# Two batches of chunks for the second normalisation of each local layer, with row statistics column-tiled on TensorE and sent through DRAM to all partitions

## Chip, cores, metric

One core of a Trainium2 chip. The metric is the time of one execution on the device, in microseconds (us). The kernel is a program written out by hand: each engine has its own list of instructions, and semaphores connect the lists.

## What is computed

The input x is (4, 1024, 128), so 4096 tokens of 128 channels. A feed-forward block of two local layers, a global attention block, and the same feed-forward block again:

```python
x = x + 0.5 * ffn(layernorm(x))        # two local layers
x = x + attn(layernorm(x))             # causal attention and a memory term
x = x + 0.5 * ffn(layernorm(x))        # the same two local layers
```

One local layer, of which there are four in one execution:

```python
h = shift_token(x)                     # upper 64 channels come from the token before
q, k, v = split(h @ wqkv); q, k = l2norm, scales, rotary_xpos
x = x + local_attention(q, k, v) @ wo  # windows of 64 tokens
h = shift_token(x)
h = (h - h.mean(-1)) / sqrt(h.var(-1) + 1e-5) * lg + lb
a, g = split(h @ w1 + b1)              # 341 hidden channels each
x = x + (a * gelu(g)) @ w2 + b2
```

The change is about the third line from the end of the second part: the mean and variance over the 128 channels of each token, between attention and the hidden layer ("the second normalisation").

## The kernel before

Activations lie channels-first, [128 channels, tokens], in `z_a` (`z_in`, the layer's input) and `z_b` (`z_out`, the sum after attention). Tokens are cut into 32 tiles of 128 (`TILE`, numbered 0 to 31 in a layer) and 8 chunks of 512 (`CHUNK`, numbered 0 to 7), so chunk m is tiles 4m to 4m+3.

`local_attention_pass` runs both layers of one feed-forward block. For tiles 0 to 27 a function `body(i, k)` on each engine interleaves stages of five different tiles: keys, queries and values of tiles ahead (L197 to L208), the softmax maxima on VectorE (L403), the exponentials on ScalarE (L330, eight a tile, called slots 0 to 7), the normalisation of the probabilities on GpSimd (L298), their transposes on TensorE (L249) with copies to SBUF (`probsT`, L351 on ScalarE and L416 on VectorE), the products with the values (L265), the head copy (L356), the output projection (L276), and the residual (L421, semaphore `z_done`). GpSimd also sums and scales the rotary parts (L285, L291), after which TensorE turns queries and keys of the tile (L219, semaphores `q_turned`, `k_turned`).

Tiles 28 to 31 are written out in `attention_end(layer)`, and there the second normalisation of all eight chunks is woven in by hand. This stretch is called the tail below. For each chunk:

- SyncE copies the shifted chunk from `z_out` to `ln_h` with two DMAs (`sp_ln_chunk`, L532 and L533); for chunk 7 VectorE and GpSimd copy the halves instead (`dve_ln_high` L519, `gp_ln_low` L525).
- TensorE multiplies by `K["centre"]`, identity minus 1/128, into a PSUM bank (L475, a full 128x512 f32 product: `pe_centre`).
- ScalarE squares that (L497), TensorE multiplies the squares by `K["mean"]`, all 1/128 (L490, `pe_var`), which gives the variance on all 128 partitions at once; ScalarE takes the logarithm (L503) and exp(-0.5 log) (L508); VectorE multiplies the centred bank by it into `z_in` (L512, `dve_ln_scale`).

After the tail come the eight chunks of the hidden layer: gate and value products (L592, L597), the rest of the hidden channels (L603, and L610 as two products on 64 columns each), Gelu on ScalarE (L630), `dve_hide` (L640), the down product (L621) and the sum on VectorE (L646). The first Gelu needs another table of activations, loaded by L979 behind the last exponential of the normalisation. Hidden-layer products wait for PSUM banks that Gelu and `dve_hide` release (`pe_await_bank`).

Each f32 product is two records (and two weight loads) in the profile. Engines take their lists in order: an instruction whose semaphore isn't there holds up all behind it on its engine.

Of the kernel before, what the change touches and what calls it, by code (L numbers as in the profile page):

```python
# [14 lines left out]
P = 128  # L15
# [83 lines left out]
LN_MOVES = ("ln_low", "ln_high")  # L99
MLP_SEMS = ("mlp_gate", "mlp_value", "mlp_gelu", "mlp_hidden", "mlp_down", "mlp_out")  # L100


LN_PAIRS = ((0, 1), (1, 0), (0, 1), (3, 4), (1, 0), (4, 3), (0, 1), (2, 7))
LN_BEHIND = {1: 0, 2: 1, 4: 2, 5: 3, 6: 4}
# [29 lines left out]
WOVEN = TILES - 4  # L134

# [4 lines left out]
def local_attention_pass(nc, C, K, W, probs, probsT, z_in, z_out, x, first):  # L140


    C.open(("pass_set", "ln_in0", "ln_in1", "ln_in2", "ln_in3", "hs_in0", "hs_in1", "hs_in2", "hs_in3", "v_in0", "v_in1", "v_in2", "v_in3"))
    with ExitStack() as ctx:
# [27 lines left out]
        ln_h, squares, rstd = ln[:, 0:4, :], ln[:, 4:6, :], ln[:, 6:8, :]  # L172
# [32 lines left out]
        def pe_project_values(pe, wait, i, k):  # L205
            wait("v_ready", i, k, 1)
            wait("z_done", i, k, 4)
            nc.tensor.matmul(ps[:, VB, :], hs[:, k % 4, :], W["wqkv"][:, i // B, 2 * INNER:3 * INNER], start=True, stop=True  # L208
                             ).then_inc(C["v_done"], 1)
# [242 lines left out]
        def ln_wait(eng, name, layer, m):  # L452
            eng.wait_ge(C[name], C.after(name, CHUNKS * (layer + 1) + m + 1))

        def ln_banks(layer, m):
            return FIRST_PAIRS[m % 3] if layer < 0 else LN_PAIRS[m]


        def pe_centre(pe, wait, layer, m):
# [4 lines left out]
            elif m == CHUNKS - 1:  # L464
                pe.wait_ge(C["ln_low"], C.after("ln_low", layer + 1))
                pe.wait_ge(C["ln_high"], C.after("ln_high", layer + 1))
            else:
                pe.wait_ge(C[f"ln_in{m % 4}"], C.after(f"ln_in{m % 4}", (32 if m % 4 == 3 else 64) * layer + 32 * (m // 4 + 1)))
                if m == 0:
                    wait("q_rotated", *t(layer, LAST))  # L470
                elif m == 3:
                    wait("max_done", *t(layer, LAST), 0, HEADS)
                else:
                    ln_wait(pe, "ln_log", layer, LN_BEHIND[m])
            nc.tensor.matmul(ps[:, centred, :], K["centre"][:, :], x[:, columns(m)] if layer < 0 else ln_h[:, m % 4, :],  # L475
                             start=True, stop=True).then_inc(C["ln_centred"], 1)

        def pe_var(pe, wait, layer, m):
# [5 lines left out]
            elif m == CHUNKS - 1:  # L484
                wait("heads_ready", *t(layer, LAST))
            elif m == 0:
                wait("k_squared", *t(layer, LAST))
            elif m != 3:
                ln_wait(pe, "ln_out", layer, LN_BEHIND[m])
# [3 lines left out]
        def act_ln_square(act, layer, m):  # L493
            ln_wait(act, "ln_centred", layer, m)
            if m >= 2:
                ln_wait(act, "ln_var", layer, m - 2)
            nc.scalar.activation(squares[:, m % 2, :], ps[:, ln_banks(layer, m)[0], :], ACT.Square).then_inc(C["ln_squared"], 1)  # L497

        def act_ln_log(act, layer, m):
            ln_wait(act, "ln_var", layer, m)  # L500
            if m >= 2:
# [13 lines left out]
        def dve_ln_high(dve, wait, layer):  # L515
            m = CHUNKS - 1
            wait("z_done", *t(layer, LAST))
            ln_wait(dve, "ln_centred", layer, m - 4)
            nc.vector.tensor_copy(ln_h[64:128, m % 4, :], z_out[64:128, columns(m, 1)]).then_inc(C["ln_high"], 1)  # L519

        def gp_ln_low(gp, wait, layer):
            m = CHUNKS - 1
            wait("z_done", *t(layer, LAST))
            ln_wait(gp, "ln_centred", layer, m - 4)
            nc.gpsimd.tensor_copy(ln_h[0:64, m % 4, :], z_out[0:64, columns(m)]).then_inc(C["ln_low"], 1)  # L525

        def sp_ln_chunk(sp, wait, layer, m):

            wait("z_done", *t(layer, 4 * m + 3))
            if m >= 4:  # L530
                ln_wait(sp, "ln_centred", layer, m - 4)
            sp.dma_start(ln_h[0:64, m % 4, :], z_out[0:64, columns(m)]).then_inc(C[f"ln_in{m % 4}"], 16)  # L532
            sp.dma_start(ln_h[64:128, m % 4, :], z_out[64:128, columns(m, 1)]).then_inc(C[f"ln_in{m % 4}"], 16)  # L533
# [55 lines left out]

        def pe_gate(pe, layer, c, j):  # L590
# [2197 lines left out]
```

## Time and profile before

| | us |
|---|---|
| three runs: median (lowest, highest) | 1970.66 (1968.64, 1971.12) |
| the profiled execution, its own time | 1968.74 |
| span of the profile | 1966.7 |
| busy: TensorE, VectorE, ScalarE, GpSimd | 1898.6, 1648.5, 1504.3, 915.3 |
| granted TensorE clock, mean | 0.986 |

The span runs from the first to the last instruction in the profile. 1968.74 is the time of that one execution; the difference of 2.0 us lies around the span. A busy TensorE isn't necessarily at its peak, as ends of products are modelled; where starts are compared, the distance between starts is the price of an instruction.

The four tails begin (first product of the normalisation) at 268.45, 589.43, about 1539 and 1860.08 us. The words "first tail" mean the one of 268.45.

### The profile page before, as it was taken

The numbers are of one execution on the slowest core, as the hardware profiler recorded it, in microseconds if no ns is written. First come the engines' busy times: TensorE is split into PE (matmuls) and PEld (weight loads), VectorE is DVE, ScalarE is ACT, GpSimd is POOL, SyncE is SP. The second block draws the span as 40 slices with busy tenths as digits, with TensorE's granted clock in tenths as the row PEclk, the third lists the DMA queues.
The fourth block names the chain that finished last, engine by engine and source line by source line (L and its number), as shares of the span: only waits on it lengthen the run. The fifth ranks groups of instructions, "written<-read, shape, count | busy, mean of one in ns | idle before, by whom it ended". The sixth has DMA issues, their size and how long they took to land. (4 is left out here: it accounts for less than half of the span.)

```text
span 1966.7 us, 53041 instructions
## 1 busy us (share of the span) xinstructions
PE 1898.6 (97%) x18494; PEld 1125.7 (57%) x18494; DVE 1648.5 (84%) x5474; ACT 1504.3 (76%) x4121; POOL 915.3 (47%) x548
## 2 busy tenths in 40 slices
PE   7999999999999989999999998899999999999998
PEld 3777763577775343434434367437777635777753
DVE  5999975899995679999999769779999659999955
ACT  5999994799997353777777754469999848999963
POOL 2788860588882040000000046337888406888800
PEclk9999999999999997999999999999999999999999
DMA  6222220112120040111111000002212201121201
GB/s 185 46 45 46 46 65 6 34 43 49 43 66 23 6 155 26 42 42 41 43 41 42 20 5 2 2 19 49 48 43 47 55 6 41 43 48 43 67 15 43
DMA packets 76107, 85.11 MB, mean 43 GB/s; under 512 B 17136, under 2 KB 50500, under 8 KB 75716
## 3 DMA queue, kind: packets, MB, share of 16 engines
q1 hardware_dynamic: 75647, 81.70, 16.6%
q8 instruction: 150, 2.46, 0.5%
q14 instruction: 114, 0.93, 0.2%
q10 hardware_dynamic: 196, 0.02, 0.0%
HBM read 21.16 MB, written 8.39 MB: 15 GB/s over the span
## 5 line engine op out<-in xcount | busy, mean ns | idle before, releaser
L330 ACT ACTIVATE probs<-probs,negmax 128x128 f32<-128x128 f32 x1024 | 399.9, 396 | 23.6 <-DVE negmax L403 22.5
L2165 ACT ACTIVATE gprobs<-ps_global 128x1024 f32<-128x1024 f32 (+3 forms) x384 | 291.4, 811 | 125.1 <-PE ps_global L1630 102.4
L285 POOL TENSOR_TENSOR rot<-rot 128x1024 f32<-128x1024 f32 x128 | 302.1, 2360 | 144.0 <-DVE rot L373 144.0
L291 POOL TENSOR_TENSOR qk<-rot,cnorm 128x1024 f32<-128x1024 f32 x128 | 243.7, 1904 | 120.2 <-POOL rot L285 92.3
L298 POOL TENSOR_TENSOR probs<-probs,iden 128x1024 f32<-128x1024 f32 x128 | 242.8, 1897 | 120.1 <-DVE iden L411 120.1
L1860 DVE TENSOR_REDUCE maxes<-ps_global 128x1 f32<-128x512 f32 (+2 forms) x384 | 222.1, 639 | 10.7 <-PE ps_global L1593 6.5
L403 DVE CUSTOM_DVE_ANT_0 probs<-ps_attn,masks 128x128 f32<-128x128 f32 x1024 | 226.0, 285 | 0.4 <-issue 0.3
L1588 PE MATMUL ps_global<-kq 48*128 48x512 bf16 (+3 forms) x768 | 196.7, 345 | 7.5 <-DVE maxes L1860 1.8
L330 ACT ACTIVATION_READ_ACCUMULATOR probs<-probs,negmax 128x1 f32 x1024 | 197.1, 192 | 0.0
L371 DVE TENSOR_TENSOR rot<-ps_attn,rotary 128x512 f32<-128x512 f32 x256 | 175.1, 684 | 2.1 <-PE ps_attn L197 1.5
L265 PEld LDWEIGHTS ps_attn<-probsT,v_first 128*64 128x64 f32 x2048 | 118.1, 136 | 98.1 <-ACT probsT L351 95.1
L2095 POOL CAST m_parts<-m_turn 32x128 bf16<-32x128 f32 x16 | 4.5, 280 | 363.6 <-DVE m_turn L1874 363.6
L1645 PE MATMUL ps_global<-gprobs,v_all 128*9 128x512 f32 (+3 forms) x1536 | 160.7, 490 | 1.7 <-ACT gprobs L2165 1.7
L249 PEld LDWEIGHTS ps_attn<-ident,probs 128*128 128x128 f32 x1024 | 117.7, 140 | 69.2 <-POOL probs L298 61.4
L630 ACT ACTIVATE ln<-ps_attn,vecs_sb 128x512 f32<-128x512 f32 (+2 forms) x96 | 65.6, 683 | 116.8 <-PE ps_attn L592 72.7
L379 DVE TENSOR_REDUCE ssq<-sq 128x16 f32<-128x1024 f32 x128 | 154.7, 1209 | 0.1
L1856 DVE CUSTOM_DVE_ANT_0 ps_global<-ps_global,later 128x384 f32<-128x384 f32 (+1 forms) x256 | 152.2, 653 | 2.7 <-PE ps_global L1588 1.7
L1588 PEld LDWEIGHTS ps_global<-kq 48*128 48x128 bf16 x768 | 58.8, 94 | 160.3 <-DVE maxes L1860 86.4
L1621 PE MATMUL ps_global<-kq 51*128 51x512 bf16 (+3 forms) x768 | 145.6, 329 | 2.3 <-ACT gprobs L2165 1.9
L219 PE MATMUL ps_attn<-ident,qk 128*128 128x128 f32 x1024 | 139.8, 279 | 5.9 <-POOL qk L291 3.9
L236 PE MATMUL ps_attn<-kT,qT 64*64 64x128 f32 x4096 | 141.3, 275 | 0.0
L265 PE MATMUL ps_attn<-probsT,v_first 128*64 128x64 f32 x2048 | 138.5, 230 | 0.7 <-ACT probsT L351 0.7
(220 smaller groups left out, 4599.4 us busy)
## 6 DMA issues: line engine op xcount, KB each, us to landing
v_first<-v_second SPq DMA_DIRECT2D x256, 128.0 KB, 2.3
hs<-z_a SPq DMA_DIRECT2D x256, 32.0 KB, 1.9
ln<-z_b SPq DMA_DIRECT2D x56, 128.0 KB, 2.4
kq<-split_scratch SPq DMA_DIRECT2D x64, 96.0 KB
kq<-split_scratch SPq DMA_DIRECT2D x64, 64.0 KB
split_scratch<-parts SPq DMA_DIRECT2D x8, 384.0 KB, 4.1
split_scratch<-gprobs SPq DMA_DIRECT2D x6, 384.0 KB, 4.1
x_tok<-in_x_dram SPq DMA_DIRECT2D x4, 512.0 KB, 6.5
```

Of the source, the lines that this page charges most:

```text
L265: last = nc.tensor.matmul(out[:, queries], v[:, k % 4, cols], probsT[:, 4 * e + pair, queries], start=True, stop=True, skip_group_check=True)
L285: nc.gpsimd.tensor_tensor(a, a, b, ALU.add).then_inc(C["rot_sum"], 1)
L291: nc.gpsimd.tensor_tensor(qk[:, k % 2, :].rearrange("p (h d) -> p h d", d=DH), rot_a[:, k % 2, :, :], cnorm[:, k % 2, :].unsqueeze(2).to_b ...
L298: nc.gpsimd.tensor_tensor(pr, pr, iden[:, k % 2, :].unsqueeze(2).to_broadcast([P, HEADS, SPAN]), ALU.mult).then_inc(C["probs_ready"], 1)
L330: last = nc.scalar.activation(probs[:, k % 2, slot, :], probs[:, k % 2, slot, :], ACT.Exp, scale=-1.0, bias=negmax[:, k % 2, slot:slot + 1 ...
L371: nc.vector.tensor_tensor(rot_a[:, k % 2, h0:h0 + HEADS, :], x, cos, ALU.mult)
L379: nc.vector.reduce_sum(ssq[:, k % 2, :], sq[:, :].rearrange("p (h d) -> p h d", d=DH), AX_X).then_inc(C["ssq_done"], 1)
L403: nc.vector.tensor_tensor_reduce(probs[:, k % 2, slot, :], ps[:, SB0 + slot // 4, (slot % 4) * SPAN:(slot % 4 + 1) * SPAN], K["masks"][:, ...
L1588: mm = nc.tensor.matmul(out, qs[buf][rows, p, tile_cols(t)], ks[buf][rows, p, CHUNK * c:CHUNK * c + w], start=True, stop=not masked_here, ...
L1645: mm = nc.tensor.matmul(ps[32 * h:32 * h + AD + 1, O0, t0 - CHUNK * c:CHUNK], v_all[:, S_TILES * (n // GROUPS) + s, GROUP * (n % GROUPS) + ...
L1860: nc.vector.reduce_max(maxes[:, n % 2, r, p0:p1, t, c], ps[:, bank_of(use), 0:len(both) * w].rearrange("q (p s) -> q p s", s=w), AX_X).the ...
L2165: nc.scalar.activation(probs[:, step % RING, 2 * p:2 * p + 2, 0:w], ps[:, S0 + 2 * p:S0 + 2 * p + 2, 0:w], ACT.Exp).then_inc(C["p2_exp"], 1)
```

## The change

Chunks 0 to 3 form batch 0, chunks 4 to 6 form batch 1 (`LN_BATCHES`). Chunk 7 keeps the old way (its source is now `last_h`). A batch goes so, b being its number:

1. Inputs. SyncE copies the shifted chunks to `inputs[m]`, for batch 0 while tiles 20 to 23 run, for batch 1 after tile 30's values, and there behind `k_turned` of tile 31, as the chunks lie in the buffer `qk`.
2. `pe_mean`: for each chunk a product with 32 columns of `K["mean"]`, each in its own quarter of the array's columns, all into one PSUM bank. Batch 0 in `body` of tile 26, batch 1 in the tail, between the transposed probabilities and the value products of tile 29.
3. `act_mean` copies the bank to SBUF; for batch 1 it stands ahead of slots 4 to 7 of tile 30's exponentials.
4. `sp_spread(…, 0)`: SyncE writes one row a chunk to DRAM, waits for it, and reads it back to all 128 partitions.
5. `centre_batch`: input minus mean, on VectorE for batch 0 (ahead of `dve_inv` of tile 29), on GpSimd for batch 1 (ahead of `gp_ln_low`).
6. `act_batch_square`, `pe_batch_var` (column-tiled again), `act_batch_log`, `act_batch_inverse`, once a batch.
7. `sp_spread(…, 1)` sends the inverse deviations the same way, and `dve_batch_scale` multiplies. Chunks 0 and 1 are scaled ahead of the residual of tile 31, chunks 4 to 6 inside the hidden layer, behind the first `dve_out`.

`first.gpsimd`, scaling of weights in the first pass alone, moves from the end of GpSimd's tail to behind tile 28's part of it. The core of the diff:

```diff
+LN_BATCHES = ((0, 1, 2, 3), (4, 5, 6))
+EARLY_MEAN = WOVEN - 2
+        def pe_mean(pe, wait, layer, b):
+            if b == 0:
+                bank = VB
+                wait("z_done", *t(layer, EARLY_MEAN - 1))
+            else:
+                bank = KB
+                wait("k_squared", *t(layer, LAST))
+            step_wait(pe, "lb_in", layer, b, moves_in(b), moves_in(b))
+            for n, m in enumerate(LN_BATCHES[b]):
+                last = nc.tensor.matmul(ps[32 * n:32 * n + 32, bank, :], K["mean"][:, 0:32], inputs[m], start=True, stop=True,
+                                        skip_group_check=True, tile_position=(0, 32 * n))
+            last.then_inc(C["lb_mean"], 1)
...
+        def centre_batch(eng, engine, layer, b):
+            step_wait(eng, "lb_spread", layer, b, spread_moves(b), 2 * spread_moves(b))
+            for m in LN_BATCHES[b]:
+                engine.tensor_tensor(inputs[m], inputs[m], spread[m], ALU.subtract).then_inc(C[f"lb_centred{b}"], 1)
...
+        def sp_spread(sp, wait, layer, b, what):
+            batch_wait(sp, ("lb_copied", "lb_rstd")[what], layer, b)
+            n = len(LN_BATCHES[b])
+            out = ln_rows[layer, b, what, 0:n, :]
+            sp.dma_start(out, rows_of[b][0:32 * n - 31:32, :]).then_inc(C[f"lb_rows{b}"], 16)
+            step_wait(sp, "lb_rows", layer, b, 16 * (what + 1), 32)
+            if b == 0:
+                sp.dma_start(ln[:, 4:8, :], out.partition_broadcast(P)).then_inc(C["lb_spread0"], 16)
+                return
+            if what == 0:
+                wait("ssq_done", *t(layer, LAST))
+            sp.dma_start(qk_flat[:, 3, :], out[0, :].partition_broadcast(P)).then_inc(C["lb_spread1"], 16)
+            sp.dma_start(sq_flat[:, :, :], out[1:3, :].partition_broadcast(P)).then_inc(C["lb_spread1"], 16)
...
 # TensorE, attention_end
                 pe_transpose_probs(pe, wait, *t(layer, 29), True)
-                pe_var(pe, wait, layer, 1)
+                pe_mean(pe, wait, layer, 1)
                 pe_values(pe, wait, *t(layer, 29), True)
...
-                pe_centre(pe, wait, layer, 7)
-                ln_wait(pe, "ln_out", layer, 6)
+                wait("max_done", *t(layer, LAST), 0, HEADS)
                 pe_gate(pe, layer, 0, 0)
-                pe_var(pe, wait, layer, 7)
                 pe_gate(pe, layer, 0, 1)
+                pe_batch_var(pe, wait, layer, 1)
                 wait("p5_read", *t(layer, LAST))
                 pe_value(pe, layer, 0, 0)
+                pe_centre(pe, wait, layer, LAST_CHUNK)
                 wait("p6_read", *t(layer, LAST))
                 pe_value(pe, layer, 0, 1)
+                batch_wait(pe, "lb_log", layer, 0)
                 pe_wide(pe, layer, 0)
+                pe_var(pe, wait, layer, LAST_CHUNK)
...
 # VectorE, attention_end
                 dve_clip_norm(dve, wait, *t(layer, 31))
+                centre_batch(dve, nc.vector, layer, 0)
                 dve_inv(dve, wait, *t(layer, 29))
...
                 dve_probsT(dve, wait, *t(layer, 31))
-                dve_ln_scale(dve, layer, 3)
-                dve_ln_scale(dve, layer, 4)
+                dve_batch_scale(dve, layer, 0)
+                dve_batch_scale(dve, layer, 1)
                 dve_residual(dve, wait, *t(layer, 31))
```

What this does to the order of instructions, in the first tail. TensorE from the output projection of tile 28 on (L276 before, L295 now), before:

```order
L276 MATMUL ps_attn<-oT,wo_sb 128x128 x4
L475 MATMUL ps_attn<-ln,centre 128x512
L249 MATMUL ps_attn<-ident,probs 128x128 x8
L490 MATMUL ps_attn<-ln,mean 128x512
L265 MATMUL ps_attn<-probsT,v_first 64x64
```

and now (L268 is what L249 was, L284 what L265 was):

```order
L295 MATMUL ps_attn<-oT,wo_sb 128x128 x4
L268 MATMUL ps_attn<-ident,probs 128x128 x8
L504 MATMUL ps_attn<-qk,mean 32x512 x3
L284 MATMUL ps_attn<-probsT,v_first 64x64
```

One chunk's centring and variance gave way to the three means of batch 1, on whose inputs the value products of tile 29 now wait.

TensorE at the start of the hidden layer, before (L592, L597, L603 are gate, value and the wide rest):

```order
L276 MATMUL ps_attn<-oT,wo_sb 128x128 x4
L490 MATMUL ps_attn<-ln,mean 128x512
L475 MATMUL ps_attn<-ln,centre 128x512
L592 MATMUL ps_attn<-z_a,w_sb 128x512
L490 MATMUL ps_attn<-ln,mean 128x512
L592 MATMUL ps_attn<-z_a,w_sb 128x512
L597 MATMUL ps_attn<-z_a,w_sb 128x512 x2
L603 MATMUL ps_attn<-z_a,w_sb 128x512
```

and now (L701, L706, L712 are those three; L587 centres chunk 7, L598 is its variance):

```order
L295 MATMUL ps_attn<-oT,wo_sb 128x128 x4
L701 MATMUL ps_attn<-z_a,w_sb 128x512 x2
L515 MATMUL ps_attn<-qk,mean 32x512
L515 MATMUL ps_attn<-sq,mean 32x512 x2
L706 MATMUL ps_attn<-z_a,w_sb 128x512
L587 MATMUL ps_attn<-late_rows,centre 128x512
L706 MATMUL ps_attn<-z_a,w_sb 128x512
L712 MATMUL ps_attn<-z_a,w_sb 128x512
L598 MATMUL ps_attn<-ln,mean 128x512
```

Chunk 7's centring moved from ahead of the first gate product to behind four of the steps.

SyncE in the first tail now, from the values of tile 30 on (L460, L461 load values; L561, L562 the inputs of batch 1; L569 writes rows to DRAM):

```order
L460 DMA v_first<-v_second 64x512
L461 DMA v_first<-v_second 64x512
L561 DMA qk<-z_b 64x512
...
L562 DMA qk<-z_b 64x512
L460 DMA v_first<-v_second 64x512
L461 DMA v_first<-v_second 64x512
L569 DMA ln_rows_first<-qT 3x512
L576 DMA qk<-ln_rows_first 128x512
L577 DMA sq<-ln_rows_first 128x1024
L569 DMA ln_rows_first<-late_rows 4x512
L572 DMA ln<-ln_rows_first 128x2048
```

Six input DMAs stand where the cut is (three pairs), and the round trip of batch 0's deviations (the last two rows) is queued behind that of batch 1's means.

## Rows read from the trace of the kernel before

**Rows 1.** Busy time by stretch: one tile, first tail, hidden layer, fourth tail
```profile
core 0: us, PE busy (x) PEld busy (x) DVE busy (x) ACT busy (x) POOL busy (x), PEclk, DMA share, GB/s
253.24:260.82 7.58, 7.58 (x96) 5.52 (x96) 7.28 (x34) 7.17 (x27) 6.11 (x4) 1.00 0.18 40
268.40:300.35 31.95, 30.06 (x299) 19.49 (x298) 15.87 (x65) 28.76 (x84) 16.58 (x11) 1.00 0.16 36
311.07:366.00 54.93, 53.97 (x129) 21.97 (x127) 33.68 (x54) 22.50 (x36) 7.00 (x4) 1.00 0.05 11
1860.03:1891.88 31.85, 30.06 (x298) 19.47 (x297) 15.86 (x65) 28.76 (x84) 11.46 (x7) 1.00 0.17 37
```
**Rows 2.** Timeline of the first tail: start us, us, engine, line, operation [idle before]
```profile
268.45 1.02 PE L475 MATMUL ps_attn<-ln,centre 128*128 128x512 f32 x2
269.31 1.04 PE L249 MATMUL ps_attn<-ident,probs 128*128 128x128 f32 x8
...
272.24 1.90 POOL L291 TENSOR_TENSOR qk<-rot,cnorm 128x1024 f32<-128x1024 f32 x1 [0.79 <-POOL rot L285]
...
274.20 1.09 PE L219 MATMUL ps_attn<-ident,qk 128*128 128x128 f32 x8 [0.58 <-POOL qk L291]
...
279.50 0.41 ACT L330 ACTIVATE probs<-probs,negmax 128x128 f32<-128x128 f32 x1
...
283.88 1.04 PE L249 MATMUL ps_attn<-ident,probs 128*128 128x128 f32 x8
...
291.33 1.04 PE L249 MATMUL ps_attn<-ident,probs 128*128 128x128 f32 x8
...
296.12 1.05 PE L276 MATMUL ps_attn<-oT,wo_sb 128*128 128x128 f32 x8
297.21 0.29 DVE L421 TENSOR_TENSOR z_b<-ps_attn,z_a 128x128 f32<-128x128 f32 x1 [2.11 <-PE ps_attn L276]
```
**Rows 3.** Timeline, same columns, from there into the hidden layer
```profile
300.35 1.10 PE L592 MATMUL ps_attn<-z_a,w_sb 128*128 128x512 f32 x2 [0.74 <-DVE z_a L512]
...
302.34 0.69 ACT L503 ACTIVATE ln<-ps_attn,ln_eps 128x512 f32<-128x512 f32 x1 [2.10 <-PE ps_attn L490]
...
305.00 1.26 ACT L630 ACTIVATE rot<-ps_attn,vecs_sb 128x512 f32<-128x512 f32 x2
...
311.07 2.74 PE L621 MATMUL ps_attn<-rot,w_sb 128*128 128x512 f32 x6
```
**Rows 4.** Timeline of a global-attention stretch: eight records are four products on separate columns
```profile
900.41 1.04 PE L1645 MATMUL ps_global<-gprobs,v_all 128*9 128x512 f32 x8
901.39 0.39 PE L1588 MATMUL ps_global<-kq 48*128 48x384 bf16 x2
```
**Rows 5.** DMA issues: engine, count, KB each, median us from issue to landing
```profile
w_sb<-in_w_dram SPq DMA_DIRECT2D x1, 704.0 KB, 5.0
probs<-in_rotary_tables_dram SPq DMA_DIRECT2D x1, 1024.0 KB, 6.3
wqkv_sb<-in_wqkv_dram SPq DMA_DIRECT2D x1, 1536.0 KB, 11.5
kq<-m_parts SPq DMA_DIRECT2D x96, 4.0 KB, 1.8
```
**Rows 6.** Input DMAs of chunks 0 to 3 in the first tail: issue ns, landing us
```profile
L533 SPq DMA_DIRECT2D ln<-z_b x4: 597/600/605, 260.5 to 264.3; - x4
...
DMA to landing us min/median/max: 2.3/2.4/3.3
```
**Rows 7.** VectorE beside GpSimd: timeline, then groups by shape (busy us, mean ns)
```profile
269.09 2.36 POOL L285 TENSOR_TENSOR rot<-rot 128x1024 f32<-128x1024 f32 x1
270.99 0.49 DVE L386 TENSOR_TENSOR newton<-inorm 128x16 f32<-128x16 f32 x1
...
L2600 DVE TENSOR_TENSOR rotary<-probs,probsT 128x512 f32<-128x512 f32 x8 | 5.0, 686 | 6.3 <-DMA probsT<-in_k_scale_dram 6.3
L388 DVE SCALAR_TENSOR_TENSOR newton<-newton,ssq 128x16 f32<-128x16 f32 x128 | 22.4, 175 | 4.4
```

More of the change, by code:

```diff
@@ new lines, in step_wait, with moves_in, spread_moves @@
+        def step_wait(eng, name, layer, b, n, per):
+            eng.wait_ge(C[f"{name}{b}"], C.after(f"{name}{b}", per * layer + n))
+        def moves_in(b):
+            return 32 * len(LN_BATCHES[b])
+        def spread_moves(b):
+            return 16 * (1 + b)
+        def pe_mean(pe, wait, layer, b):
[10 more added lines that the diff above has]
+            last.then_inc(C["lb_mean"], 1)
@@ new lines, in pe_batch_var @@
+        def pe_batch_var(pe, wait, layer, b):
+            if b == 0:
+                wait("q_rotated", *t(layer, LAST))
+            else:
+                batch_wait(pe, "lb_copied", layer, 1)
+            chunk_wait(pe, "lb_squared", layer, LN_BATCHES[b][-1])
+            for n, m in enumerate(LN_BATCHES[b]):
+                last = nc.tensor.matmul(ps[32 * n:32 * n + 32, (QB, KB)[b], :], K["mean"][:, 0:32], spread[m], start=True, stop=True,
+                                        skip_group_check=True, tile_position=(0, 32 * n))
+            last.then_inc(C["lb_var"], 1)
@@ new lines, in rows_used, with act_mean, act_batch_square @@
+        def rows_used(b):
+            return slice(0, 32 * len(LN_BATCHES[b]))
+        def act_mean(act, wait, layer, b):
+            if b:
+                wait("scores_done", *t(layer, LAST - 1))
+            batch_wait(act, "lb_mean", layer, b)
+            nc.scalar.copy(rows_of[b][rows_used(b), :], ps[rows_used(b), (VB, KB)[b], :]).then_inc(C["lb_copied"], 1)
+        def act_batch_square(act, layer, m):
+            b = m // 4
+            step_wait(act, "lb_centred", layer, b, m - 4 * b + 1, len(LN_BATCHES[b]))
+            nc.scalar.activation(spread[m], inputs[m], ACT.Square).then_inc(C["lb_squared"], 1)
@@ L500, in act_ln_log @@
             ln_wait(act, "ln_var", layer, m)
-            if m >= 2:
+            if layer < 0 and m >= 2:
                 ln_wait(act, "ln_out", layer, m - 2)
@@ L671, in body @@
                     pe_transpose_probs(pe, wait, i, k, ahead(i, k, 2))
+                if early_mean is not None:
+                    pe_mean(pe, wait, early_mean, 0)
                 if ahead(i, k, 4):
@@ L687, in attention_end @@
             def attention_end(layer):
-                pe_centre(pe, wait, layer, 0)
                 pe_transpose_probs(pe, wait, *t(layer, 28), True)
@@ L864, in attention_end @@
                         gp_normalise(gp, wait, *t(layer, tile + 1))
-                if first is not None and layer == 0:
-                    first.gpsimd(gp)
+                    if first is not None and layer == 0 and tile == WOVEN:
+                        first.gpsimd(gp)
+                centre_batch(gp, nc.gpsimd, layer, 1)
                 gp_ln_low(gp, wait, layer)
@@ L906, in body @@
                     act_probsT(act, wait, i, k)
+                if early_mean is not None:
+                    act_mean(act, wait, early_mean, 0)
                 if ahead(i, k, 4):
```

221 lines of the change are left out of this document (120 added, 101 removed).

## The prediction

> **What bounds the kernel now.** I read the busy time by stretch first. In a steady tile TensorE is busy for all of 7.58 us, and VectorE (7.28) and ScalarE (7.17) nearly so; in a tail TensorE is busy for 30.06 of 31.95 us, and the fourth tail repeats the first; in the hidden layer, from the first down product on, it is busy for 53.97 of 54.93 [rows 1]. So TensorE's list sets the pace nearly everywhere, and the change touches one stretch of 32 us, four times. Then the timeline of the first tail: its stations are the turning of queries and keys of tile 31 at 274.20, the transposed probabilities of tiles 30 and 31 at 283.88 and 291.33, the last output projection at 296.12 and its residual at 297.21 [rows 2]; then the first gate product at 300.35, the last logarithm at 302.34, first Gelu at 305.00, first down product at 311.07 [rows 3]. From the down product on TensorE is full, so whatever moves that start moves the end. I put the four layers equal, and work out the first.
>
> **What is removed and added.** One full product costs 0.86 us (268.45 to the next start at 269.31 [rows 2]). Seven centrings and seven variances go: 14 x 0.86 = 12.0 us of TensorE. Four groups of column-tiled products come. The trace has four f32 products of 512 on separate column quarters: 0.98 us from their start to the next [rows 4], so 3.9 us in all, of which one group falls into tile 26 and three into tail and hidden layer. TensorE's net in the tail is -9.1 us. If nothing new were waited for, this would be the result. But the list is shorter only; the new steps carry waits, and I walk them with the durations of the rows. Times are those of the first tail, without the shift of tile 26, which is added at the end.
>
> **Tile 26.** TensorE is full [rows 1], so the group of 0.98 us ahead of the query projection pushes the tile. VectorE and ScalarE have 0.30 and 0.41 us of slack (7.58 less their busy times); ScalarE's copy, about 0.5 us, hides in part behind the late queries. I take +0.7; the ends are 0.3 (half is caught up in tile 27) and 1.0.
>
> **Centring on VectorE.** A 128x512 f32 operation on two SBUF operands took 686 ns [rows 7], so four are 2.8 us ahead of `dve_inv` of tile 29. The means of batch 0 were copied some 15 us earlier, so their round trip is over. But VectorE's two-operand instructions wait for a GpSimd instruction under way: L386, 16 elements, took 0.49 us and ended at 271.48, when GpSimd's L285 ended (269.09 + 2.36), while L388 of the same size takes 175 ns [rows 7]. The first centring now meets GpSimd's scaling of tile 31 (272.24, 1.90 us [rows 2]). Either goes first; if VectorE does, the scaling and with it the turning of queries and keys starts 0.67 us late, at 274.9. I take that. `dve_inv` of tile 29 moves to 276.9, from which only tile 29 suffers, and less than from the next step.
>
> **First new wait: inputs of batch 1.** They wait for the turning to end, 274.9 + 1.0. SyncE then issues six DMAs 0.64 us apart (600 ns each and a gap), and each lands 2.3 to 3.3 us after its issue [rows 6]: 275.9 + 0.1 + 5 x 0.64 + 2.6 = 281.8. Till then TensorE stands at the means of batch 1, with the value products of tile 29 behind them, and ScalarE at `act_mean`, with slots 4 to 7 of tile 30 behind it. Means 1.15 to ScalarE, copy 0.5: slot 4 starts at 283.4, not 279.50 [rows 2]: 3.9 late. Four exponentials of 0.39, VectorE's reciprocal and GpSimd's 1.9 us later the transposes of tile 30 start at 287.5, not 283.88 (+3.6). Behind them TensorE has the variances of batch 0 (0.87 + 0.98, with the hand-over 289.5), and ScalarE their logarithm, slot 4, the inverse and slots 5 to 7 of tile 31: 0.59 + 0.52 + 4 x 0.39 = 2.7, so 292.1. The transposes of tile 31 follow at 294.7, not 291.33 (+3.4). Here the missing products first pay: from transposes to output projection are 3.7 us of latency instead of 4.8, as two centrings and one variance no longer stand between: 298.4 against 296.12 (+2.3).
>
> **Second new wait: the deviations of batch 0.** Their inverse is issued at 290.5. SyncE writes 8 KB (4 KB landed in 1.8 [rows 5]; I take 2.2), waits, and reads 1 MB. For that 704 KB gave 5.0, 1024 KB 6.3 and 1536 KB 11.5 [rows 5]; the first and the last bound it. I take 5.5, nearer 1024 KB but without that one's queue of loads. It lands at 290.5 + 0.65 + 2.2 + 5.5 = 298.9. Two scalings of 0.69 stand ahead of the residual of tile 31: 300.2, not 297.21 (+3.0).
> The Trainium skill (DMA: Bandwidth & Descriptors, Anatomy of one DMA) gives a fit of 2.0 us plus bytes over 436 GB/s, measured on another queue; by it 1 MB would be an estimated 4.4 us and the tail 0.4 us shorter. The row of 1024 KB speaks for more.
>
> **Third: chunk 7's place.** It is the chain to the first Gelu. Before, residual to Gelu took 7.8 us [rows 2, 3]. Now TensorE puts two gates, the variances of batch 1 and one value product ahead of its centring, and one value and the wide product ahead of its variance. First gate 299.7; centring 299.7 + 3 x 0.86 + 0.98 = 303.2; variance 303.2 + 3 x 0.86 = 305.8; then 1.06 to the logarithm, and from there 2.66 to Gelu as in rows 3 (302.34 to 305.00): 309.4 to 309.5, against 305.00, so +4.4. The first down product follows 6.0 later, at 315.4, against 311.07 (+4.3). The hidden layer's added scalings, 3 x 0.69 on VectorE, are hidden: it is busy for 33.68 of 54.93 us [rows 1]. Without that cover they would cost 2.1 us.
>
> **Sum.** (4.3 + 0.7) x 4 = +20 us. On the profiled execution's 1968.74 that is 1988.7; the median shown is 1.9 above that execution, so I predict **1991 us**, 1.0% slower. About 0.2%, 4 us, is what a measurement of this kernel tells from no change. Other costs: batch 0's inputs, 8 DMAs in tiles 20 to 23, are early by over 10 us; the weights' scaling on GpSimd (16.58 - 11.46 = 5.1 us, first tail against fourth [rows 1]) falls where that engine is idle half of the time, and would otherwise hold up tile 30's probabilities in one tail of four; removed ScalarE work (5 logarithms, 5 exponentials) lies beside waits now.
>
> Own range of this case: per tail, landing 2.3 or 3.3 instead of 2.6 gives -0.3 or +0.7, the broadcast 5.0 or 7.5 gives -0.2 or +2, tile 26 gives -0.4 or +0.3, GpSimd first at the lock -0.7, and my walk of the old tail came 0.9 us short of the trace, which leaves 1 us either way. So 1978 to 2004.
>
> **Rivals.**
> - **TensorE's sum decides** (faster). The tail is 94% full [rows 1]; its 9.1 us come off, less 0.7 in tile 26: -8.4 x 4 = -34, 1937 us. For it: nothing but that list is full now. Against: slot 4 of tile 30 may start no later than 279.5, so batch 1's inputs would have to land by about 278, 2.2 us after they can be issued at all, and six take 3.2 to issue. It decides if these land by 278 and the broadcast by 295; then the tail could be shorter. Chance 0.16, most of it for results between this and no change.
> - **The waits cancel with the products taken out** (within 0.2%): the landing at 281.8 is absorbed as tile 30's exponentials catch up, and the closing chain costs 1 us a layer, 1970 us. Chance 0.07.
> - **The broadcast is slow.** Every one of 128 partitions reads the same 8 KB of DRAM, which no row shows. At 10 us, near the row of 1536 KB, the residual of tile 31 comes 4.5 later still: (9 + 0.7) x 4 = +39, 2010 us. It decides from 5.5 us on, as VectorE stands at it. Chance 0.14.
> - **Column tiles don't overlap.** At 4 x 0.86 = 3.4 us a group, the tail has +5 and tile 26 +2.5: +50 us, 2020. Rows 4 are against it. Chance 0.03. The Trainium skill (TensorEngine Tiling (Array Packing), Key Properties) states that changing the tiling mode drains TensorE. It names no price; the group of rows 4 stands between products of other modes and shows 0.98 with it.
>
> **How the numbers follow.** Forecast 0.60, rivals 0.16, 0.07, 0.14, 0.03. Faster by over 0.2%: 0.16; within: 0.07; slower: 0.77. The range of 1968 to 2006 holds the forecast, no change and the near parts of the other two, and leaves out about 0.2.
>
> **What would show it.** The means of batch 1 start near 282.5, with TensorE idle for over 2 us before them, released by a DMA; ScalarE idle before the copy; VectorE idle for 1 us or more before the first scaling, released by a DMA; first Gelu 9 us behind the last residual; tail to first down product 47.5 us, where it was 42.6 (268.45 to 311.07 [rows 2, 3]). The prediction is wrong if the means start before 279, or if the time to the down product is under 43.

## The result, and the profile after

| us | before | after |
|---|---|---|
| median (lowest to highest) | 1970.89 (1968.64 to 1971.4) | 2007.45 (2005.55 to 2011.71) |
| profiled execution, its own time | 1968.74 | 2005.55 |
| span of the profile | 1966.7 | 2003.8 |
| granted TensorE clock, mean | 0.986 | 0.970 |

The changed kernel takes 1.0196 times as long (95% interval 1.0184 to 1.0208; the two medians alone give 1.0186). By the medians it is 36.6 us slower, where +20 was forecast. TensorE's busy time fell by 4.7 us only (1898.6 to 1893.9), though by the prices of the prediction its list had become 32 us shorter (four times the 12.0 that went, less the 3.9 that came). The page of the changed kernel, its busy times and the clock granted in 40 slices:
```profile
span 2003.8 us, 53048 instructions
...
PE 1893.9 (95%) x18494; PEld 1124.9 (56%) x18494; DVE 1663.5 (83%) x5490; ACT 1486.7 (74%) x4089; POOL 931.5 (46%) x560
...
PEclk9999989999998996999999999999999899999989
```
The kernel before shows one slice below 9, in the global pass (a 7 in slice 16 of 50 us). Here four more are, slices 6, 13, 32 and 39, and each holds one of the four local tails. Busy time by stretch shows the same tails whole, from the transposes of tile 28 to the first down product: the first (271.64 to 318.78), the hidden layer behind it, and the fourth; then the third; then the same stretch of the first tail before.
```profile
core 0: us, PE busy (x) PEld busy (x) DVE busy (x) ACT busy (x) POOL busy (x), PEclk, DMA share, GB/s
271.64:318.78 47.14, 35.79 (x315) 22.31 (x316) 22.76 (x68) 29.89 (x83) 19.84 (x13) 0.89 0.27 80
318.78:371.00 52.22, 51.58 (x124) 21.20 (x123) 33.06 (x53) 21.94 (x36) 4.71 (x2) 1.00 0.02 5
1890.80:1939.30 48.50, 37.63 (x303) 23.39 (x304) 20.61 (x64) 27.74 (x74) 12.44 (x8) 0.79 0.25 77
```
```profile
1560.80:1608.90 48.10, 36.35 (x274) 21.37 (x267) 20.15 (x60) 26.88 (x69) 11.76 (x8) 0.82 0.26 78
```
```profile
269.31:311.07 41.76, 39.87 (x321) 23.47 (x321) 20.37 (x66) 35.12 (x91) 15.67 (x10) 1.00 0.12 27
```
The first tail grew from 41.76 to 47.14 us while TensorE's busy time in it fell by 4.1: it now stands idle for 11.4 us. And the granted clock is 0.89, 0.82 and 0.79 in the tails shown, where it was 1.00 before. Stretch by stretch it is at half of full speed (1.2 GHz) or at full (2.4 GHz), never between. Behind the first down product of this layer it is back at 1.00, and nothing more is lost there.

The timeline of the first tail after, beside [rows 2] and [rows 3] (start us, us, engine, line, operation, idle before):
```profile
276.98 1.09 PE L238 MATMUL ps_attn<-ident,qk 128*128 128x128 f32 x8 [0.74 <-POOL qk L310]
...
280.82 1.09 PE L268 MATMUL ps_attn<-ident,probs 128*128 128x128 f32 x8 [1.85 <-POOL probs L317]
281.22 0.60 SPq L562 DMA_DIRECT2D qk<-z_b  x1
...
283.73 1.93 PE L504 MATMUL ps_attn<-qk,mean 128*32 128x512 f32 x6 [1.82 <-DMA qk<-z_b]
...
285.75 0.58 ACT L526 COPY qT<-ps_attn 96x512 f32<-96x512 f32 x1 [2.25 <-PE ps_attn L504]
286.24 0.40 ACT L349 ACTIVATE probs<-probs,negmax 128x128 f32<-128x128 f32 x1
...
290.17 1.08 PE L268 MATMUL ps_attn<-ident,probs 128*128 128x128 f32 x8
...
295.65 0.33 SPq L572 DMA_DIRECT2D ln<-ln_rows_first  x1
...
297.40 1.85 PE L268 MATMUL ps_attn<-ident,probs 128*128 128x128 f32 x8
...
300.37 1.73 DVE L553 TENSOR_TENSOR z_a<-ln 128x512 f32<-128x512 f32 x2 [0.39 <-DMA ln<-ln_rows_first]
...
303.12 0.29 DVE L440 TENSOR_TENSOR z_b<-ps_attn,z_a 128x128 f32<-128x128 f32 x1 [1.03 <-PE ps_attn L295]
...
306.69 1.02 PE L587 MATMUL ps_attn<-late_rows,centre 128*128 128x512 f32 x2
...
309.26 1.02 PE L598 MATMUL ps_attn<-ln,mean 128*128 128x512 f32 x2
...
312.98 1.27 ACT L740 ACTIVATE rot<-ps_attn,vecs_sb 128x512 f32<-128x512 f32 x2
...
318.78 1.45 PE L731 MATMUL ps_attn<-rot,w_sb 128*128 128x512 f32 x3
```
Four new things are to be seen: TensorE stands for 1.85 us ahead of the transposes of tile 29, whose normalisation on GpSimd is late, and then 1.82 us for batch 1's inputs ahead of its means; transposes that take 1.85 us where the same eight took 1.08 seven us earlier (the same products at half clock); and 9.9 us from the last residual to the first Gelu, where it was 7.8.

**Where the 36.6 us came from.** A layer's growth is how much later its first down product starts than before, less how much later its tile 0 already was. The last column is the time that the clock spent at half within the tail.

| layer | growth, us | at half clock, us |
|---|---|---|
| first | 5.8 | 10.2 |
| second | 6.5 | 10.2 |
| third | 9.8 | 17.1 |
| fourth | 10.6 | 20.5 |

They sum to 32.6. Another 1.9 was there before tile 0 of the first layer, 1.1 came in the second layer's hidden part, and 1.5 in the global pass: 37.1, the difference of the two spans.

### The profile page after: what moved, and what is told of

It reads as the page before. It is cut to its first block and busy times, and to the rows that moved or that the text cites. A ratio compares the mean times of both kernels' runs of the same rounds, so it can differ in the third digit from the quotient of the medians.

```text
span 2003.8 us, 53048 instructions
## 1 busy us (share of the span) xinstructions
PE 1893.9 (95%) x18494; PEld 1124.9 (56%) x18494; DVE 1663.5 (83%) x5490; ACT 1486.7 (74%) x4089; POOL 931.5 (46%) x560
## 5 line engine op out<-in xcount | busy, mean ns | idle before, releaser
L284 PEld LDWEIGHTS ps_attn<-probsT,v_first 128*64 128x64 f32 x2048 | 121.4, 139 | 104.6 <-ACT probsT L370 90.6
L268 PEld LDWEIGHTS ps_attn<-ident,probs 128*128 128x128 f32 x1024 | 120.7, 144 | 75.1 <-POOL probs L317 66.8
L295 PE MATMUL ps_attn<-oT,wo_sb 128*128 128x128 f32 x1024 | 140.3, 281 | 11.5 <-ACT oT L375 11.5
L268 PE MATMUL ps_attn<-ident,probs 128*128 128x128 f32 x1024 | 137.9, 279 | 10.7 <-POOL probs L317 10.7
L284 PE MATMUL ps_attn<-probsT,v_first 128*64 128x64 f32 x2048 | 142.7, 235 | 5.0 <-issue 3.3
```

The costliest lines, as they stand in the source:

```text
L268: last = nc.tensor.transpose(ps[:, b, s * TILE:(s + 1) * TILE], probs[:, k % 2, 4 * e + s, :], K["ident"][:, :])
L284: last = nc.tensor.matmul(out[:, queries], v[:, k % 4, cols], probsT[:, 4 * e + pair, queries], start=True, stop=True, skip_group_check=True)
```

## Experiments

Each ratio is to the kernel before, run on the same chip. Gains in us are from the 2007.45 of the changed kernel. Beside that the kernel before had a median of 1970.89, and beside the experiments 1969.3 to 1969.8, so about 1 to 1.5 us of each gain owes nothing to the edit. "Growth" is that of the table above, read from the profiled execution.

**Work for TensorE where it stood idle.**
```
+def pe_fill(pe, bank, n):
+    for _ in range(n):
+        nc.tensor.matmul(ps[:, bank, 0:256], K["centre"][:, :], W["wqkv"][:, 0, 0:256], start=True, stop=True)
```


> The changed kernel, and in each local tail 12 products of 128x256 whose results nothing reads, put on TensorE where it stood idle: 1 behind the scores of tile 30, 3 behind the output projection of tile 28, 2 ahead of the means of batch 1, 4 behind the values of tile 30, 2 around the values of tile 31. Nothing that the kernel needs is left out. Theory (the new waits and the granted clock together make the 36.6 us): the clock stays at 1.00 in the tails, the means of batch 1 take 1.07 us instead of 1.93, the transposes of tile 31 take 1.0 instead of 1.85, and of the 36.6 us about 10 go: 1997 us. Rival A (the waits alone; the slow products lie inside waits that are there anyway): the clock comes back in the page and the time stays within 2 us of 2007. Rival B (the extra products delay the needed ones by more than the clock gives back): above 2009.

1994.95 us, ratio 1.013 (1.0116 to 1.0143): 12.5 below the changed kernel, near the 10 of the theory. The third tail in this kernel, then its means, which waited for the same DMA:
```profile
1559.20:1601.20 42.00, 35.04 (x292) 20.92 (x283) 19.51 (x60) 26.52 (x67) 11.59 (x8) 1.00 0.28 89
```
```profile
1567.37 1.06 PE L504 MATMUL ps_attn<-qk,mean 128*32 128x512 f32 x6 [0.97 <-DMA qk<-z_b]
```
First and third layer kept the clock at 1.00 and grew by 4.3 and 4.1 us. Over the four layers growth fell from 32.6 to 22.5. Second and fourth still had 3.4 us at half each, and grew by 7.1 and 7.0. Part of that was no clock: in the fourth tail the means started 3.9 us after the issue of the last input DMA (1890.56 to 1894.45), where 2.4 was usual, and in the second the broadcast of batch 0's deviations took 6.9 us, where the other three took 4.5 to 4.6:
```profile
626.79 1.29 DVE L557 TENSOR_TENSOR z_a<-ln 128x512 f32<-128x512 f32 x2 [3.47 <-DMA ln<-ln_rows_first]
```
In the other tails of this kernel VectorE stood 1.1 to 1.2 us there, where in the changed kernel it stood 0.2 to 0.4. So once the products ahead of it are fast, the broadcast is waited for.

**Batch 1's inputs not behind the transposes.**
```
+raw = inputs[0:4] + [rot[:, n, :] for n in (0, 1, 4)]
-    wait("k_turned", *t(layer, LAST))
+    wait("qk_ready", *t(layer, LAST - 1))
```


> The changed kernel, but the inputs of batch 1 come into three rows of rot that are free once tile 30's q and k are scaled, and wait for that instead of the last transposes of q and k; the centring reads them there and writes its result where the inputs lay before. Same instructions. Theory (the first new wait is on the path): the inputs land near 275.5 in layer 0, the means of batch 1 follow the transposes of tile 29 at 281.9 instead of 283.73, the end exps of tile 30 and all behind them come 1.8 us earlier, and more where the clock no longer falls: 4 x 1.8 = 7, up to 10 with the clock: 1999 us. Rival A (a later wait, the broadcast of the deviations or chunk 7's place, sets the end of the tail whatever the first wait does): within 2 us of 2007.

1988.0 us, ratio 1.0095 (1.008 to 1.0111): 19.5 below, twice what was expected. The first wait is on the path, and with it went most of the clock's fall: three of four tails now spend 3.4 us at half clock (10 to 20 before) and grow by 3.4 to 3.8. The first went the other way: 13.7 us at half (10.2 before), and a growth of 7.4 (5.8). What of the gain is wait and what clock, this run alone doesn't part.

**The means of batch 1 later in both lists.**
```
-pe_mean(1); pe_values(29); pe_scores(31)
+pe_values(29); pe_scores(31); pe_mean(1)
-act_mean(1); act_exp(30, 4 to 7); act_heads(29)
+act_exp(30, 4 to 7); act_heads(29); act_mean(1)
```


> The changed kernel with the four-part product group of batch 1's means moved on TensorE from ahead of the values of tile 29 to behind the scores of tile 31, and its copy on ScalarE from ahead of the end exps of tile 30 to behind the head copy of tile 29. Nothing else. Theory (the first wait costs because work of the attention stands behind it on two engines): the values of tile 29 start at 283.0 instead of 285.6 and the end exps of tile 30 at 282.9 instead of 286.2, transposes of tile 30 near 287.5; the tail ends about 3 us earlier in each layer: 4 x 3 = 12: 1995 us. Rival A (a later wait sets the end): within 2 us of 2007. Rival B (means later, so their broadcast and the centring of batch 1 are late for the squares): the gain in the tail is lost at the first Gelu: 2005.

1995.15 us, ratio 1.013 (1.0108 to 1.0151): the theory's total, but not by its steps, and its executions spread from 1987.6 to 2001.1. In the first tail the transposes of tiles 30 and 31 came 2.2 us earlier than in the changed kernel (287.97 and 295.14), near the theory's 3; but then the gates ran at half clock, and the layer grew by more. The four tails had 13.7, 13.7, 3.4 and 10.2 us at half clock and grew by 7.8, 7.3, 4.0 and 6.2, where the changed kernel grew by 5.8, 6.5, 9.8 and 10.6. That the total met the 1995 is luck.

**Chunk 7's products ahead of the values** (in short form; the three calls marked + stood further behind, among and behind the value products).
```
 pe_gate(0, 0)
+pe_centre(7); pe_batch_var(1)
 pe_gate(0, 1)
+pe_var(7)
 pe_value(0, 0); pe_value(0, 1); pe_wide(0)
```


> The changed kernel with chunk 7's centring product on TensorE directly behind the first gate, its variance directly behind the second gate, and the two value products and the wide product behind those; on ScalarE chunk 7's square ahead of the logarithm of batch 1. Nothing else. Theory (chunk 7's new place is on the path of the first Gelu): the centring starts near 304.8 instead of 306.7 and the variance near 307 instead of 309.3 in layer 0, the first Gelu near 310.4 instead of 313.0: 4 x 2.6 = 10: 1997 us. Rival A (the first Gelu waits for the table load, and that for the batch's logarithms whatever chunk 7 does): within 2 us of 2007. Rival B (the hidden layer is then bound by the value products that now come later): gain under 1 us a layer, 2004.

1991.62 us, ratio 1.0116 (1.0102 to 1.013): 15.8 below. In the fourth tail:
```profile
1911.24 0.29 DVE L440 TENSOR_TENSOR z_b<-ps_attn,z_a 128x128 f32<-128x128 f32 x1 [0.99 <-PE ps_attn L295]
...
1912.51 1.12 PE L587 MATMUL ps_attn<-late_rows,centre 128*128 128x512 f32 x2 [0.45 <-POOL late_rows L633]
...
1915.52 1.02 PE L598 MATMUL ps_attn<-ln,mean 128*128 128x512 f32 x2
...
1919.24 1.27 ACT L740 ACTIVATE rot<-ps_attn,vecs_sb 128x512 f32<-128x512 f32 x2
```
Residual to Gelu is 8.1, 8.0, 8.0 and 8.0 us in the four tails. In the changed kernel it is 9.9 twice, and 11.1 and 10.8 in the third and fourth, where some of it ran at half clock. So chunk 7's place is 1.7 to 1.9 us a layer at full clock, less than the 2.6 of the theory and about 7.5 of the 15.8. The rest goes with the clock: third and fourth tail had 10.2 and 3.4 us at half, where they had 17.1 and 20.5; the first had more, 13.7 for 10.2.

**The three edits together.**

> The three single edits together: inputs of batch 1 in free rows of rot, chunk 7's products ahead of the values on TensorE, and 12 products of 128x256 with unread results in TensorE's idle stretches. Theory (three costs: the first wait, chunk 7's place, the clock): in the layers of the single runs that kept the clock at 1.00, the first wait's removal leaves a layer 3.0 us behind the kernel before and chunk 7's place is worth 1.9 to 2 of these; so 4 x 1.1 = 4.3, and the global pass and the start 2 to 3 as in every run: 1970 + 7 = 1977 us (range 1974 to 1981), and no half clock in any tail. Rival A (the gains of the single runs add: 12.5 + 19.5 + 15.8 = 48 off 2007.5): 1960. Rival B (a wait that the three hid comes up, the broadcast of the deviations first of all): idle VectorE before the first scaling grows from 0.4 us to over 1.5, and the time stays above 1983.

1975.95 us, ratio 1.0032 (1.002 to 1.0045), within the theory's range. No tail falls below 1.00; the layers grow by 1.0, 1.5, 0.7 and 1.4. The gains of the single runs don't add (rival A), because each had also been credited with some of the same falls. At full clock the changed order costs a layer 4.2 us (e1_fill) and this one 1.15; with 1.9 for chunk 7's place that leaves the first wait an estimated 1.2 a layer. Rival B's wait is there too, though not its time: VectorE stands 1.1, 2.2, 1.3 and 1.3 us before the first scaling of the four tails.

**A version in another order.** It keeps the second edit, puts chunk 7's two products ahead of both gates, and moves more: centring of batch 0 behind the probability copy of tile 29, the batch's logarithm and exponential behind tile 31's exps, the last residual ahead of the scalings. VectorE's part, in short form:
```
-centre_batch(0); dve_inv(29); dve_max(30); dve_residual(28); dve_probsT(29)
+dve_inv(29); dve_max(30); dve_residual(28); dve_probsT(29); centre_batch(0)
-dve_batch_scale(0); dve_batch_scale(1); dve_residual(31)
+dve_residual(31); dve_ln_high(); dve_batch_scale(0); dve_batch_scale(1)
```


> A version to beat both: inputs of batch 1 in free rows of rot; centring of batch 0 on VectorE behind the probability copy of tile 29 instead of ahead of the inverse of tile 29, its squares behind the head copy of tile 29; logarithm and exponential of batch 0 behind the exps and the head copy of tiles 31 and 30; residual of tile 31 and chunk 7's copy ahead of the first scalings; chunk 7's centring and variance ahead of the gates. No added products. Theory (the centring ahead of the inverse of tile 29 costs 2 to 2.5 us of the chain of exps, the logarithms 1.3, chunk 7's place 2 and more): without a fall of the clock each layer would be about 1 to 2 us shorter than before, 1968; with falls as in the single runs (8 to 12 us in all) about 1977. Rival A (the tail is bound by the broadcast of the deviations, which now leaves later): VectorE idles over 1 us at the first scaling, above 1983. Rival B (the clock falls in none of the tails since no wait is left): 1968 or less, the same as e7_orderfill.

1965.08 us, ratio 0.9978 (0.9969 to 0.9987), faster than the kernel before and at the time of rival B, though one tail still fell. Three of its tails hold the clock at 1.00 with no product added:
```profile
1538.00:1579.00 41.00, 34.03 (x334) 21.33 (x331) 23.23 (x87) 32.05 (x89) 16.29 (x10) 1.00 0.34 98
```
TensorE is idle for 7.0 of 41 us here and the clock stays, with all column-tiled groups still there; in the second tail it is idle for 6.8 of 40.8 us and the clock falls. So neither the groups nor this much idle time decide it by themselves. The layers change by -2.2, -0.8 (the one with 3.4 us at half), -2.5 and -2.0.

**The same with added products.**

> e6_order and 10 products of 128x256 with unread results in each tail's idle stretches of TensorE: 1 behind the output projection of tile 28, 3 behind that of tile 29, 4 behind the values of tile 30, 2 around those of tile 31. Theory: the clock stays at 1.00 in the tails and the time is 5 to 12 us below e6_order: 1968 (range 1963 to 1974). Rival A (the idle stretches are short enough that the clock stays up without them): equal to e6_order within 2 us. Rival B (the added products are in the way of the needed ones): above e6_order.

1963.2 us, ratio 0.9969 (0.9958 to 0.9981): the lowest of all, 0.3% below the kernel before. The 1.9 us below e6_order are less than can be told apart (the two intervals overlap) and less than the theory's 5 to 12: rival A is nearer.

**The group at tile 26 twice.**
```
-for n, m in enumerate(LN_BATCHES[b]):
+for n, m in [*enumerate(LN_BATCHES[b])] * (2 - b):
```


> The changed kernel with the group of four products of batch 0's means at tile 26 issued twice (the second time over the same results). Nothing else. The group took 0.98 us on TensorE and tile 26 ended 1.0 us later than before in every layer. Theory (TensorE is the bound of a tile in the woven stretch, and the group's whole length is added): another 1.0 us a layer: 2011.5 us. Rival A (what tile 26 pays is ScalarE's copy of the means and its place between the exps; the products lie beside other work): within 1.5 us of 2007.5.

2003.89 us, ratio 1.0172 (1.0158 to 1.0186). That is 3.6 below the changed kernel's median, but 1.3 of it stands between the medians of the kernel before too, and the two intervals overlap: it is clear that the time did not rise by 4, and not clear that it fell. Rival A's band is missed by 2.1 us. The group itself did as the theory said; all 16 records in a row, where there were 8 of 604 ns in 1.1 us:
```profile
L504 PE MATMUL ps_attn<-ln,mean 128*32 128x512 f32 x16 | 1.9, 598 | 0.0
```
Tile 26 ended 1.9 us later than before in three layers (2.0 in the fourth), after 1.0 (1.2) with one group. But the tails, shifted by 0.9 us, met other falls of the clock: 20.5 us at half in the first tail (growth 11.0), 10.2 in each other (7.2, 6.7, 7.3). Together 32.2 us, of which the added groups are 3.5; without them 28.7, against 32.6. What an edit adds in one place can thus be outweighed by how long the clock falls elsewhere.

**The centring alone, and put back.** The first moves only the centring and its squares in the changed kernel; the second puts the centring back in e6_order.

> The changed kernel with one thing alone moved: the centring of batch 0 on VectorE from ahead of the inverse of tile 29 to behind the probability copy of tile 29, and its four squares on ScalarE behind the head copy of tile 29. Theory (centring costs 2.8 us of VectorE ahead of tile 30's max, and its collision with GpSimd's scaling 0.7; but the first wait, the inputs of batch 1, hangs on the scaling of q and k alone, so of the 3.5 us only the 0.7 and what lies between can show): the scaling of q and k of tile 31 is not held up, the means of batch 1 come 0.7 us earlier, the exps of tile 30 that wait for max come 2 us earlier and then stand before the means: 1 us a layer and some of the clock: 2000 us (range 1994 to 2005). Rival A (the centring is the main cost): 4 x 2.8 = 11 and the clock, 1993 or less. Rival B (the means alone pace the tail): within 2 us of 2007.

> e6_order with the centring of batch 0 alone put back ahead of the inverse of tile 29. Theory (with the first wait gone the centring is on the path at its full length, 2.8 us and the collision): 2 to 3 us a layer and about 3 of clock: 1965 + 8 to 14 = 1976 us. Rival (tile 30's exps have slack there, since the exps of tile 31 and the squares behind them set the end): 1967 or less.

2002.88 us, ratio 1.0171 (1.0158 to 1.0184), and 1972.61, ratio 1.0022 (1.0014 to 1.0031). With the first wait there, moving the centring gave 4.6 us by the medians (3.0 when each is taken from the kernel before beside it), and only 1.5 in the growth of the four layers: 1.1, -0.2, 0.3 and 0.4. Half clock in the tails was 3.4, 10.2, 17.1 and 17.1 us. Without the first wait, putting it back cost 7.5 us by the medians and 9.7 in the layers (2.0, 1.6, 2.3, and 3.8 in the one whose clock fell), about the theory's 8 to 14. So at full clock the centring is about 2 us a layer, and the first wait had covered it.

**The means of batch 0 in the tail.**

> e6_order with the means of batch 0 (four products, copy, rows, broadcast) moved from tile 26 into the tail, behind the transposes of tile 28 on TensorE and behind its probability copy on ScalarE, in the bank of the queries; and in each second layer the scalings of chunks 4 to 6 spread over three chunks of the hidden layer. Theory (the group costs its 1.0 us only where TensorE bounds the tiles; the tail has room; the three scalings together cost the second layer of the first pass 1.07 us): 4 x 0.7 + 1 = 3.8 less than e6_order: 1961 us. Rival A (the broadcast of these means, now issued near 275, lands after the centring's turn and holds VectorE up): 1966 or above. Rival B (ScalarE's copy costs the tail what TensorE saves): 1964.

> e11_tailmean with the 10 added products of e7_orderfill in each tail's idle stretches of TensorE. Theory (the order of e11 leaves little idle time, so the clock falls rarely): 1 to 2 us below e11_tailmean: 1959.5. Rival A (no fall is left to prevent; the added products hold up the output projection of tile 30 by up to 1 us): equal to e11 or above it.

1968.35 us, ratio 0.9999 (0.9989 to 1.0009), and 1965.13, ratio 0.9978 (0.9969 to 0.9987). Rival A: the 1.0 us of tile 26 is saved, but VectorE stands for the broadcast, with the inverse of tile 30 behind it:
```profile
1548.82 2.50 DVE L549 TENSOR_TENSOR ln<-ln 128x512 f32<-128x512 f32 x4 [1.52 <-DMA ln<-ln_rows_second]
```
All four tails fell to half for 3.4 us; the added products undid that and took 3.2 us off, where rival A of that run expected no gain. The spread scalings did what was expected: the second layer's 1.1 us were gone in both runs.

## Why the prediction was wrong in size

The direction held, and most of the steps; in the first tail they can be compared one by one, less 2.6 us: the 1.6 by which the kernel was late ahead of tile 26, and the 1.0 of that tile.

- **Tile 26**: +1.0, not +0.7, the upper end; doubling the group gave 0.9 more. Nothing of it was caught up.
- **The lock**: it is there, and VectorE went first, as I took it, but for less. Its first centring took the usual 0.69 us, GpSimd's scaling of tile 31 started 0.2 us behind it and took 2.22 instead of 1.90, and the second centring then stood behind that scaling, which the sum had left out:
```profile
274.48 0.69 DVE L548 TENSOR_TENSOR ln<-ln 128x512 f32<-128x512 f32 x1
275.08 2.39 DVE L548 TENSOR_TENSOR ln<-ln 128x512 f32<-128x512 f32 x1
...
274.70 2.22 POOL L310 TENSOR_TENSOR qk<-rot,cnorm 128x1024 f32<-128x1024 f32 x1 [0.80 <-POOL rot L304]
```
So the turning started at 276.98, less the shift 274.4, not at 274.9. The four centrings took 4.2 us instead of 2.8, which tile 29 and the exps of tile 30 felt; behind the first wait that cost little (e9_centre), without it about 2 us a layer (e10_back).
- **First wait**: means at 281.1 (forecast 281.8; the turning was 0.5 earlier and the landing 0.2 shorter), slot 4 of tile 30 at 283.6 (283.4), transposes of tile 30 at 287.6 (287.5), of tile 31 at 294.8 (294.7). The agreement from slot 4 on is partly luck: the means took 1.93 us at half clock instead of 1.06, which made up for the 0.7.
- **Second wait**: hardly one in the changed kernel. The first scaling started at 297.8, where 298.9 was forecast for the landing: the broadcast was issued 0.3 us sooner than forecast and landed after 4.7 us, not 5.5. VectorE waited 1.4 us for it over all four tails together (group by line, 16 scalings), and the residual of tile 31 was held by TensorE, whose transposes ran at half clock. That the residual came at 300.5, forecast 300.2, is therefore luck. Where the clock stayed up the wait showed: 1.1 to 3.5 us a tail in e1_fill, 1.1 to 2.2 in e5_three. For the four broadcasts of deviations, which landed after 4.5 to 4.75 us, the fit in the Trainium skill (DMA: Bandwidth & Descriptors, Anatomy of one DMA), an estimated 4.4 us, was nearer than my 5.5; for the four of means, 5.1 to 6.0 us, it was not.
```profile
L553 DVE TENSOR_TENSOR z_a<-ln 128x512 f32<-128x512 f32 x16 | 13.3, 872 | 1.5 <-DMA ln<-ln_rows_first 0.8 <-DMA ln<-ln_rows_second 0.6
```
- **Third**: residual to Gelu 9.9 us, forecast 9.2 (300.2 to 309.4); e4_chunk7 got 1.7 to 1.9 of it back. The first down product came at 318.78 - 2.6 = 316.2, forecast 315.4.

Of the signs named beforehand, TensorE's idle time before the means (1.82 us, named as over 2) and ScalarE's before the copy came about as said, VectorE's of 1 us before the first scaling did not (0.4), and the tail to the first down product took 47.7 us (318.78 - 2.6 - 268.45), where 47.5 was named.

So in the first layer the walk is 0.8 us short. **The step that failed** is "I put the four layers equal, and work out the first", and with it that each product was put at its duration at full clock: the fall of the clock was put at nothing, without a reason. The walk gives 5.0 us a layer, and where e1_fill kept the clock at 1.00 a layer grew by 4.1 to 4.3. So at full clock the walk is 0.8 us too long, and that it came so near in the first layer is luck: by that comparison half clock added about 1.6 there. In the changed kernel the layers grew by 5.8, 6.5, 9.8 and 10.6, with 10 to 20 us at half clock each. Against four times 4.2 that is 16 us more. I had read "PEclk 1.00" in every tail [rows 1] as a property of the tail. Those rows showed it only for a TensorE busy for 94% of the tail; the new order leaves it busy for 76% (35.79 of 47.14 us), and no row told what the clock would do there.

The prediction's own ends don't add to its range either. They sum to -2.6 and +4.0 us a layer, which is 1981 to 2007 and not 1978 to 2004, and none of them is the clock.

Of the 37.1 us between the spans, then: the waits with full clock make about 17, tile 26's 4 among them (with the three edits together 4.6 are left); the clock in the tails about 16, of which added products alone brought back 10 in the layers and 11 to 12.5 in the time; the second layer's hidden part 1.1; and 3.4 us lie ahead of the first layer and in the global pass. In the second layer's hidden part the cover named for the three scalings (33.68 of 54.93 us of VectorE [rows 1], read in the first layer) was thinner. VectorE makes the decay tables there too, and the fourth layer, without them, lost nothing, so they are the likely reason, though no run leaves them out. The 3.4 us vary from run to run (-1.3 to 2.3 and -0.5 to 1.8) and in part follow stretches of half clock there; what sets them stays open. So does why a given tail falls for 3 or for 20 us.

The rival "TensorE's sum decides" was wrong for the order as written. With the waits moved away, e6_order and e7_orderfill earn about 2 us a layer of the 9.1 that had been taken from TensorE's list in the tail.

## What to carry to other kernels

Taking work from the busiest engine pays only where nothing new is waited for in its place: walk the list with the new waits, and count how long that engine will stand. If it is TensorE, price its products at both clock levels in the range, since slower products cost here about as much again as the waits. Keep a transfer's release off the last instruction that happens to free its buffer: with other rows for the inputs more than half of the loss was gone.

Judge an edit of a microsecond by its place in the timeline, and not by the total alone, while the clock falls in some stretches and not in others: doubling a group added its 0.9 us to every layer, and the total did not rise.

## What the runs showed of the hardware

- The granted clock went from 1.00 to 0.5 in single stretches of 3.4 to 10.2 us, in tails in which TensorE was idle for 11 to 12 of 47 to 48.5 us, though never for more than 2.4 us at a time; it came back by itself. Products whose results nobody reads, about 0.5 us each in gaps that were idle anyway, prevented most of it: 6.8 us at half in the four tails of e1_fill, 58 in those of the changed kernel. What the chip looks at to decide this no run here shows, and e6_order, idle for 7 of 41 us in each tail, kept the clock in three of four.
- At half clock six column-tiled products took 1.93 us instead of 1.06, and eight transposes 1.85 instead of 1.08.
- VectorE's centrings and GpSimd's scaling of tile 31 held each other up, with the same times in all four tails: the second centring took 2.39 us, ending 0.5 us behind the scaling, where the others took 0.68 to 0.69, and the scaling took 2.22 instead of 1.90.
- A read of 8 KB of DRAM by all 128 partitions (1 MB) had a median of 5.3 and 4.9 us in the two passes. Each median mixes two broadcasts of means (5.1 to 6.0 us) and two of deviations (4.5 to 4.75). The last line is of all eight:
```profile
ln<-ln_rows_first SPq DMA_DIRECT2D x4, 1024.0 KB, 5.3
ln<-ln_rows_second SPq DMA_DIRECT2D x4, 1024.0 KB, 4.9
...
DMA to landing us min/median/max: 4.5/4.9/6.0
```
